# Row maxima of two heads at once in two row groups of TensorE, and the low halves of the probabilities on GpSimd alone

## The reference

```python
q = (x @ Wq).reshape(b, s, N_HEADS, HEAD_DIM)
k = (x @ Wk).reshape(b, s, N_HEADS, HEAD_DIM)
v = (x @ Wv).reshape(b, s, N_HEADS, HEAD_DIM)
dot = jnp.einsum('bihd,bkhd->bhik', q, k)
w = jax.nn.softmax(dot / jnp.sqrt(jnp.float32(HEAD_DIM)), axis=-1)
a = jnp.einsum('bhij,bjhd->bihd', w, v)
a = a.reshape(b, s, N_HEADS * HEAD_DIM)
return a @ Wo + bo
```

## Time and profile before

| | |
|---|---|
| median of three runs | 991.6 us (991.33 to 992.09) |
| profiled execution | 990.12 us |
| its span, first to last instruction | 988.3 us |
| TensorE's mean granted clock | 0.979 of full speed |
| prologue, until the first score matmul | 71.6 us |
| attention loop, until its last normalisation | 732.7 us |
| the rest, norms and experts | 255 us |

### The profile page before, as it was taken

The page is one execution under the profiler, slowest core; times in us unless marked ns, Lnnn a source line. Parts: engine busy times, 40 slices in busy tenths (PEclk is TensorE's granted clock), DMA queues, the critical chain, the costliest instruction groups (busy, mean ns, idle before and its releaser), DMA issues. The chain is left out here.

```text
span 988.3 us, 22724 instructions
## 1 busy us (share of the span) xinstructions
PE 943.2 (95%) x9760; PEld 756.8 (77%) x9760; DVE 793.6 (80%) x1111; ACT 665.0 (67%) x818; POOL 516.5 (52%) x277
## 2 busy tenths in 40 slices
PE   6779999999999999999999999999987999999996
PEld 2337887888787887888888788777866888888885
DVE  5677999999999999899999999999887555454455
ACT  3338887888888888887887878887877222222226
POOL 3307777777777777677777777777860000000000
PEclk9898999999999999999999999999996999999998
DMA  7993616336063360724516245160010000000001
GB/s 201 237 249 85 141 27 146 80 75 135 27 153 66 94 130 26 159 53 102 125 36 153 47 114 113 42 153 3 5 46 1 1 23 23 23 23 23 23 1 43
DMA packets 47395, 79.21 MB, mean 80 GB/s; under 512 B 5056, under 2 KB 31168, under 8 KB 47168
## 3 DMA queue, kind: packets, MB, share of 16 engines
q1 hardware_dynamic: 30144, 69.17, 29.9%
q10 hardware_dynamic: 17152, 8.59, 3.7%
HBM read 17.77 MB, written 9.50 MB: 28 GB/s over the span
## 5 line engine op out<-in xcount | busy, mean ns | idle before, releaser
L462 POOL TENSOR_TENSOR pl<-p,ph 128x896 f16<-128x896 f32 x256 | 485.9, 1900 | 212.2 <-ACT ph L373 212.2
L498 DVE TENSOR_REDUCE mx<-mps 128x1 f32<-128x1024 f32 x256 | 311.7, 1218 | 49.9 <-PE mps L232 49.4
L372 ACT ACTIVATE p<-sps 128x1024 f32<-128x1024 f32 x256 | 263.9, 1031 | 118.6 <-PE sps L221 116.2
L373 ACT ACTIVATE ph<-sps 128x1024 f16<-128x1024 f32 x256 | 262.2, 1024 | 0.0
L294 PEld LDWEIGHTS ops<-vbuf,ph 128*128 128x128 f16 x2048 | 186.9, 96 | 73.3 <-issue 59.1
L502 DVE TENSOR_TENSOR pl<-p,ph 128x128 f16<-128x128 f32 x256 | 240.8, 943 | 2.1 <-ACT ph L373 2.1
L294 PE MATMUL ops<-vbuf,ph 128*128 128x65 f16 x2048 | 217.1, 194 | 2.2 <-DVE ao L540 2.0
L296 PE MATMUL ops<-vbuf,ph 128*128 128x64 f16 x2048 | 215.1, 195 | 0.0
L298 PE MATMUL ops<-vbuf,pl 128*128 128x65 f16 x2048 | 213.9, 192 | 0.0
L220 PE MATMUL sps<-q_hh,k_hl 128*128 128x512 f32 x512 | 205.6, 402 | 0.5 <-ACT ph L373 0.5
L221 PE MATMUL sps<-q_lm,k_h 65*128 65x512 f32 x512 | 204.2, 399 | 0.0
(11 more groups left out here) (122 smaller groups left out, 1014.7 us busy)
## 6 DMA issues: line engine op xcount, KB each, us to landing
q_hh<-hi SPq DMA_DIRECT2D x64, 256.0 KB, 4.6
v_dram<-vt ACTq DMA_DIRECT2D x16, 516.0 KB, 9.4
vbuf<-v_dram SPq DMA_DIRECT2D x16, 516.0 KB, 3.3
q_lm<-lo SPq DMA_DIRECT2D x32, 256.0 KB, 4.9
k_hl<-hi SPq DMA_DIRECT2D x32, 256.0 KB, 5.2
k_hl<-lo SPq DMA_DIRECT2D x32, 256.0 KB, 5.1
k_h<-hi SPq DMA_DIRECT2D x32, 256.0 KB, 5.4
w<-in_w1T SPq DMA_DIRECT2D x8, 352.0 KB, 2.9
```

The lines of the kernel that those rows point to most:

```text
L372: nc.scalar.activation(p32[:, q % 4, :], sps[:, buf % 2, :], ACT.Exp, bias=EXP_BIAS, scale=SCALE)
L373: nc.scalar.activation(ph[:, q % 4, :], sps[:, buf % 2, :], ACT.Exp, bias=EXP_BIAS, scale=SCALE).then_inc(s_exp, 1)
L462: nc.gpsimd.tensor_tensor(pl[:, c % 4, 0:POOL_COLS], p32[:, c % 4, 0:POOL_COLS], ph[:, c % 4, 0:POOL_COLS], ALU.subtract).then_inc(s_subp, 1)
L498: nc.vector.tensor_reduce(mx[:, slot, qt:qt + 1], mps[:], AX.X, ALU.max).then_inc(s_mx, 1)
```

## The change

- `maxima` takes both heads of a pair at once: two matmuls of 512 columns and 64 rows each, head 0 from partitions 0 to 63 of `hi` and head 1 from 64 to 127. An item is 128 queries by one half of the keys, for both heads. It reads `hi` and not the spread copies, so it no longer waits for the DMAs of `spread_head`, and `hi` has two buffers.
- The reduction gives two columns, into `mxh`. After the 16th item of a pair a small reduction over the two halves gives `mx`, 16 columns, which are turned, negated and sent as one DMA for both heads. `LEAD_M` is 24, so 24 items are in the prologue (`early_items`).
- That DMA moves from ScalarE's queue to SyncE's (`send_maxima`): in the prologue behind `spread_head(1, 1)`, in the loop between the two `spread_head` of a pair.
- `low_parts` is GpSimd's alone, with 1024 columns; VectorE's is gone.
- `JOBS`: one `maxima` job a pair, in slot 9, and the projections in slots 1, 3, 5 and 7.

```diff
-LEAD_M = 14
+LEAD_M = 24
-JOBS = {1: ("maxima", 1), 2: ("project", 0), 4: ("project", 1), 6: ("project", 2), 8: ("project", 3),
-        10: ("maxima", 0), 11: ("turn", 0), 12: ("add", 0), 13: ("turn", 1), 14: ("add", 1)}
+JOBS = {1: ("project", 0), 3: ("project", 1), 5: ("project", 2), 7: ("project", 3), 9: ("maxima", 0),
+        11: ("turn", 0), 12: ("add", 0), 13: ("turn", 1), 14: ("add", 1)}
...
+def early_items(t):
+
+    return range(max(0, 3 * (t - 1) // 2 - 1), max(0, 3 * t // 2 - 1)) if t < T + 1 else range(3 * T // 2 - 1, LEAD_M)
...
+            def send_maxima(par, jobs):
+                sp.wait_ge(s_used, jobs)
+                sp.dma_start(q_lm[HD:HD + 1, par, :, :].bitcast(F32), negm[:].bitcast(F32)).then_inc(s_negm, 16)
...
             for a in range(2):
                 sp.wait_ge(s_head[a], 96)
                 spread_head(1, a)
+            send_maxima(0, PRO_MISC)
...
                     spread_head(par, 0)
 
+                    for turned in maxima_turned:
+                        send_maxima(1 - par, turned)
                     sp.wait_ge(s_scores, head_scored[1])
                     sp.wait_ge(s_head[1], head_spread)
                     spread_head(par, 1)
...
-                    pe.wait_ge(s_negm, 16 * head + 16)
+                    pe.wait_ge(s_negm, 16 * pair + 16)
...
-                for kh in range(2):
-                    mm = nc.tensor.matmul(mps[:, kh * 512:(kh + 1) * 512], q_hh[:, par, a, qt * P:(qt + 1) * P],
-                                          k_hl[:, par, a, kh * 512:(kh + 1) * 512], start=True, stop=True)
+                for a in range(2):
+                    r = slice(HD * a, HD * a + HD)
+                    mm = nc.tensor.matmul(mps[:, a * 512:(a + 1) * 512], hi[r, pair % 2, 0, qt * P:(qt + 1) * P],
+                                          hi[r, pair % 2, 1, half * 512:(half + 1) * 512], start=True, stop=True)
                 mm.then_inc(s_maxmm, 1)
...
-                pe.wait_ge(s_subv, n + 1)
                 pe.wait_ge(s_subp, n + 1)
...
-                nc.gpsimd.tensor_tensor(pl[:, c % 4, 0:POOL_COLS], p32[:, c % 4, 0:POOL_COLS],
-                                        ph[:, c % 4, 0:POOL_COLS], ALU.subtract).then_inc(s_subp, 1)
+                nc.gpsimd.tensor_tensor(pl[:, c % 4, :], p32[:, c % 4, :], ph[:, c % 4, :],
+                                        ALU.subtract).then_inc(s_subp, 1)
...
-                nc.vector.tensor_reduce(mx[:, slot, qt:qt + 1], mps[:], AX.X, ALU.max).then_inc(s_mx, 1)
+                nc.vector.tensor_reduce(mxh[:, pair % 2, half, :, qt], mps[:].rearrange("p (a k) -> p a k", a=2), AX.X,
+                                        ALU.max).then_inc(s_mx, 1)
+                if i == PCH - 1:
+                    dve.wait_ge(s_mx, item + 1)
+                    nc.vector.tensor_reduce(mx[:], mxh[:, pair % 2].rearrange("p h a t -> p (a t) h"), AX.X,
+                                            ALU.max).then_inc(s_most, 1)
```

More of the change, by code:

```diff
@@ L24 @@
 V_TOP = 32768.0
-POOL_COLS = 896
 CH = 8
@@ L43, in jobs_of @@
     left = [(slot, kind, k) for slot, (kind, k) in JOBS.items()
-            if not (last and (kind == "project" or (par == 1 and (kind, k) == ("maxima", 0))))]
+            if not (last and (kind == "project" or (par == 1 and kind == "maxima")))]
     return {slot: (kind, k, number) for number, (slot, kind, k) in enumerate(left)}
@@ L182, in turn_of_pairs @@
                     sp.dma_start(mem["wo"][:, par, :], io["Wo"][wo_row:wo_row + P, :]).then_inc(s_wo, 16)
+                    maxima_turned = [first_job(last, pp, par) + number + 1
+                                     for kind, k, number in jobs_of(last, par).values() if kind == "maxima"]
                     if last:
+                        for turned in maxima_turned:
+                            send_maxima(1 - par, turned)
                         continue
@@ L210, in scores @@
                 if first_of_head is not None:
-                    pair, head = first_of_head
+                    pair = first_of_head
                     pe.wait_ge(s_head[a], 96 * pair + 96)
-                    pe.wait_ge(s_negm, 16 * head + 16)
+                    pe.wait_ge(s_negm, 16 * pair + 16)
                 buf = c % 2
@@ L313, in _ @@
                     project_early(1, t - P1_TILE, misc[:])
[L314 to L322, removed]
+                for item in early_items(t):
+                    if item == 0:
+                        pe.wait_ge(s_used, 4)
+                    maxima(item)
+                    if item == PCH:
+                        pe.wait_ge(s_ident, 1)
+                        turn_maxima(PRO_MISC - 1, 0)
             pe.wait_ge(s_vlo, 2 * T)
@@ L325, in _ @@
             pe.wait_ge(s_init, 1)
-            scores(0, 0, 0, None, (0, 0))
+            scores(0, 0, 0, None, 0)
             scores(0, 0, 1, None, None)
@@ L335, in turn_of_pairs @@
                         n = PCH * pp + s
[L337 to L340, removed]
+                        if n + LEAD_M < PAIRS * PCH:
+                            maxima(n + LEAD_M)
                         over, t = divmod(s + LEAD_S, PCH)
@@ L373, in exps, with round_piece @@
                 nc.scalar.activation(ph[:, q % 4, :], sps[:, buf % 2, :], ACT.Exp, bias=EXP_BIAS, scale=SCALE).then_inc(s_exp, 1)
[L375 to L383, removed]
+            def round_piece(par, k, job, spread, src=misc[:]):
                 if spread is not None and k == 0:
@@ L585, in turn_of_pairs @@
                         if kind == "maxima":
-                            negate_maxima(k, job + number, 32 * pp + 16)
+                            negate_maxima(job + number, pp + 1)
                         if kind == "add" and s in JOBS:
                             add_output(1 - par, k, job + number)
-                        if within(last, par, s + LEAD_M):
-                            reduce_max(ma, qt, n + LEAD_M)
+                        if n + LEAD_M < PAIRS * PCH:
+                            reduce_max(n + LEAD_M)
                         if kind == "add" and s not in JOBS:
@@ L593, in turn_of_pairs @@
                         if kind == "project":
-                            rest_of_piece(k, job + number, 4 * pp + 9 + k)
+                            rest_of_piece(par, k, 4 * pp + 9 + k)
                         if par == 1 and s == 11 and not last:
                             rest_of_weights(it + 2)
-                        if within(last, par, s + 1):
-                            low_parts((s + 1) % CH, n + 1)
                     normalise(par, 1, 1, 4 * pp + 3)
```

89 lines of the change are left out of this document (42 added, 47 removed).

## The result

| | before | changed |
|---|---|---|
| median (four runs each) | 991.81 us (991.33 to 992.09) | 1032.16 us (1030.28 to 1032.34) |
| ratio, 95% interval | | 1.0403 (1.0385 to 1.0421): slower |
| profiled execution, and its span | 990.12, 988.3 | 1032.14, 1030.3 |
| first score matmul | 71.61 | 90.56 |
| last normalisation of the attention | 732.73 | 774.60 |

A forecast was written before the change was run, and what follows sets the result against it. The prediction took TensorE's stream as the bound. From 990.1 us, low halves -5, block +5 and late start +12.4 gave 1002.5, or 1004 us on the median's scale; own range 985 to 1031, eight in ten 968 to 1066.

The forecast's parts named there:

- The bound: Attention loop: TensorE's stream fills the whole period of 41.5 us a pair of heads, with next to nothing idle.
- Low halves: Low parts all on GpSimd at 2.17 us a call: 5 us gained, 3 from waits for VectorE, 2 from queued normalisations.
- The tail: Last 24 steps, without maxima on TensorE: GpSimd sets the rate, 49 to 53 us against 52, put at 0.
- The block: Maxima matmuls to scores in each loop step: 0.56 us instead of 0.54, over 232 steps 5 us lost.
- (A): Rival: halving the array for the maxima costs nothing, block 0.41 us, total 975 us; chance 0.30.
- (B): Rival: a full pause twice a step around the half-array maxima, block 0.81 us, total 1062 us; chance 0.28.
- (C): Rival: the two maxima matmuls don't run side by side, block stays 0.54, total 999; within the forecast's 0.36.
- The loop's start: First score at 84 us, 12.4 later, since the first negm DMA queues on SyncE behind pair 1's spread.
- (D): Rival: the start isn't late, as the spread gets ahead; 12 us less, 992; chance 0.06 shared with another rival.
- The same DMA in the loop: negm DMA behind head 0's spread in the loop: no wait for a block of 0.56, 6 us for 0.41.
- (E): Rival: GpSimd becomes the bound, from 2.45 us a call on, priced 2.17; chance 0.06 shared with another rival.

The follow-up runs named there:

- run 1: Changed kernel with both maxima matmuls reading all 128 rows instead of 64 each, so not a head's maxima: 999.25 us.
- run 11: Kernel before with only the low halves changed, all 1024 columns on GpSimd and none on VectorE: 987.93 us, ratio 0.9941.
- run 10: Changed kernel with the low halves split again, 896 columns on GpSimd and 128 on VectorE: 1033.88 us, ratio 1.0391.
- run 2: Changed kernel with both half-array maxima matmuls in one row group, partitions 0 to 63: 1091.27 us.
- run 3: Changed kernel with head 1's maxima matmul moved behind the step's scores, a second half-array visit in each step: 1220.99 us.
- run 4: Changed kernel with each block's two row-group maxima matmuls issued twice, four in a visit: 1085.1 us.
- run 5: Changed kernel with the first negm DMA issued by ScalarE in tile 14 of the prologue, not by SyncE: 1027.28 us, ratio 1.0335.
- run 8: Changed kernel with early maxima spread two a tile over tiles 3 to 14 and the first negm DMA issued by ScalarE after tile 13: 1018.03 us, ratio 1.0235.
- run 6: Changed kernel with the prologue's early maxima spread out, two a tile from tile 3 to 14, DMA still on SyncE: 1032.37 us.

## Why the prediction was wrong, by its own steps

**The bound** was right: TensorE's stream before and after, and each change of a spacing in it shows in the period.

**The sum as measured.** 990.1, +30.2 for the row groups (2.10 / 16 a step by run 1, 232 steps), -4.5 for the other 0.31 us a pair that run 1 is under the kernel before, +19.0 for the start and -2.9 for the last 24 steps make 1031.9, where 1032.1 was measured. In the forecast these are +5, -5, +12.4 and 0. Two terms failed: the price of the block and the start.

**Low halves.** The price of 2.17 us a call was right (2.14). The gain of 5 us is there in the kernel before (run 11: 4.6 between the first and last normalisation), but in the main not where I put it. I laid 3 us of it to the values' waits for VectorE's `pl`, and run 11 has as long waits for GpSimd's. It was the turning of the maxima that waited for VectorE, so the right size is partly luck. In the changed kernel the turning comes two steps behind the last reduction, with or without VectorE's share of the low halves (0.03 behind the values in run 10 too): the rest of the change had already removed that wait. That is why run 10 shows nothing. What is left of VectorE's load doesn't show either: in run 10 it has 1.22 + 1.00 = 2.22 us a step under TensorE's 2.32, and 23.2 of the 23.3 us that TensorE waits there for reductions lie in the first 110 us. The tail was put at 0, out of 49 to 53 us against 52; it came at the lower end and gave 3.

**The block** is the term that failed most: +5 forecast, +30.2 measured (25.8 after what the other parts gave back). The step that failed is the price of going to half the array and back, which I took as two pauses of 0.03 to 0.04 and one bare load. Its parts, measured behind value matmuls in the changed kernel, with run 1 as the whole-array case:

| | forecast | measured |
|---|---|---|
| the `mps` matmuls to the scores | 0.41, with the second load 0.11 behind the first, plus a pause | 0.42; the second load costs nothing (one stream is 0.23; that the other 0.19 is a bare load of 0.11 and a pause of 0.08 is argued) |
| pause on entering | 0.03 to 0.04 | 0.12 - 0.03 = 0.09 |
| scores' first load laid bare | 0.08 | 0.34 - 0.23 = 0.11, behind the first score |
| sum | 0.56 | 0.62 |
| the same after a projection, after another job | 0.56 at all steps | 0.43 + 0.10 + 0.11 = 0.64, 0.42 + 0.17 + 0.11 = 0.70 |
| the same before | 0.54 at all steps | 0.54, but 0.46 after a projection |

The running side by side was undervalued and the switch too, and these two partly cancel: behind values the new sum is off by 0.06. The rest is that the steps are not alike. I had the 0.46 in the earlier trace rows and used it only to price a load. In a pair 4 steps follow a projection and cost 0.18 more than before, 5 follow another job and cost 0.16 more, and 7 follow values and cost 0.08 more: 2.08 us, against the 2.10 of run 1. Of the 25 us by which this term was off, some 14 are the 0.06, 6 the projections and 6 the other jobs.

Put as a trade: side by side saves one stream, 0.23. A visit to the half array costs 0.31 more than whole-array maxima after values, 0.39 more after a turning or an adding and 0.41 more after a projection. Neither (A) nor (B) is true. (A) has the saving right and denies the price; (B) takes the pause as the whole tail of a matmul, 0.16, twice: on the way in it is 0.09 or 0.10, and 0.17 only behind the short 32-bit matmuls of the jobs. Why it is longer there stays open. (C) is excluded by the common start of the two matmuls, and by run 2. The Trainium skill, "TensorEngine Tiling (Array Packing)", Key Properties, says that tiles run at the same time and that a change of mode drains the engine. The runs agree with the first half, 0.42 against 0.66 for two row groups against one. With the second they are in keeping, since a price is paid once a visit (runs 3 and 4), but it is well under the 0.81 that the prediction made of a full drain.

**The loop's start.** +12.4 forecast, +19.0 measured, by the mechanism that I named and one that I set too low. TensorE does wait for the DMA to `q_lm`, and that DMA does stand behind the spread. But the spread started 8.2 later (63.69 for 55.49), not 2, and `negm` was issued at 84.36, not at 77.3. I had made the removed wait for pair 0's spread pay for the 10 extra reductions. That wait was 8.0 us before and is gone, but the wait for reductions went from 5.9 to 21.4. Of the 19 us, the queue of this one DMA is 6.6 by itself (run 5). Another 5.1 come back only when the early maxima are also spread out and the DMA is sent as soon as `negm` is ready (run 8); spreading them alone gives nothing, since the queue then holds the first score (run 6). The last 7.2 no run took away. (D) fell: nothing lightened the prologue. A share that I didn't have at all is the clock: 15.1 us of the loop at the lower level where there were 8.0. Run 8 had 3.8 us less of loop for 11.7 us less of it, so the 7.1 are worth some 2 us (an estimate), in the loop and not in the 19.0.

**The same DMA in the loop.** Right: after the first, TensorE's matmuls wait 0.4 us in all at the scores. (E) fell with 2.14 us a call.

## What to carry to other kernels

Running two half-array matmuls side by side saves one stream, but each visit to the half array costs a fixed price. Here 0.23 was saved and 0.31 to 0.41 paid, so it would take two such pairs in a visit to win, and then by little, by run 4's 0.24 for a second pair (an estimate; it would need twice the room of `mps`, and wasn't run). When a spacing in a stream depends on what stands ahead of it, price the edit against each of its kinds, not against the commonest. And where a change gives a start more work, follow the DMA that the first wait names back through its queue: issuing one small DMA when its data was ready, with the early maxima placed so that it was ready soon, gave a third of the loss back. A wait that a part of the change removes may be one that another part removes too: try each part in both kernels, as runs 10 and 11 do.

## What the hardware showed that I had not expected

- Weight loads to two row groups of 64 rows go at once: two in one record of 0.19, where two whole-array loads start 0.11 apart (changed kernel, and the earlier trace rows).
- A 64-row matmul of 512 columns saves no time over a 128-row one: a second one in the same row group adds 0.24 to a visit (run 2), and so does a second pair (run 4), where a 128-row one takes 0.23.
- Going from the whole array to half adds 0.09 to the spacing behind 16-bit value matmuls, 0.10 behind projections and scores, and 0.17 behind the 128-column 32-bit matmuls of a turning or an adding. Coming back adds 0.11 behind the first score. Within a visit some 0.19 go beside the stream of 0.23.
